# The scratch tensor u in natural order (channel, batch, time): one run of 8 KB per channel stored, each channel's rows loaded by two DMAs of 64 batches

## The reference

```
# x (64, 128, 2048); condition (64,) in 0..15; weights (16, 128, 128); length (64,)
W = weights[condition]
u = x + einsum('bct,bcd->bdt', x, W)        # a 128x128 matrix per batch mixes the channels
dt = exp(log_dt);  A = -exp(log_A_real) + 1j*A_imag;  dtA = A*dt
Ct = (C[...,0] + 1j*C[...,1]) * (exp(dtA) - 1)/A
K  = 2*real(einsum('hn,hnl->hl', Ct, exp(dtA[:,:,None]*arange(2048))))   # one long filter per channel, 64 modes
y  = causal_convolution(u, K) + u*D[:,None]  # along time, done with an FFT
out = u + y * (arange(2048) < length[:,None])[:,None,:]
```

## Time and profile before

| | us |
|---|---|
| median of three runs | 1077.04 |
| lowest and highest run | 1073.87, 1077.26 |
| span of the profiled execution | 1073.5 |
| mixing stage, DMA-paced part | 18 to about 250 |
| last batches of mixing, paced by PE | 250 to 313 |
| hand-over from mixing to the main stage | 313 to 334 |
| first slots, with the stores of kept halves | 334 to 402 |
| steady slots | 402 to 1050 |

### The profile page before, as it was taken

One profiled execution on the slowest core, in us unless ns is written; L12 is line 12 of the kernel. 1 busy time (PEld: TensorE's weight loads), 2 busy tenths in 40 slices (PEclk: granted clock), 3 DMA queues, 4 the chain that ended last, 5 costly groups with the idle time before them and its releaser, 6 DMA issues.

```text
span 1073.5 us, 30051 instructions
## 1 busy us (share of the span) xinstructions
PE 1004.2 (94%) x11612; PEld 741.1 (69%) x11612; DVE 717.1 (67%) x1647; ACT 580.4 (54%) x1230; POOL 654.8 (61%) x1377
## 2 busy tenths in 40 slices
PE   7977779778999999999999999999999999999998
PEld 4333234233347887888888888888888888888886
DVE  3988950000006877788788788778778778888875
ACT  2643444344535555566566556556655656656654
POOL 3211051201207887888888888888888888888740
PEclk9999999899999999999999999999999999999999
DMA  8999999999989999999999999999999999999994
GB/s 323 424 421 424 423 422 423 363 424 424 424 314 326 292 281 261 252 230 229 232 225 234 223 233 235 224 234 222 230 224 225 226 212 250 224 223 229 237 220 124
DMA packets 169630, 305.01 MB, mean 284 GB/s; under 512 B 78274, under 2 KB 111426, under 8 KB 161298
## 3 DMA queue, kind: packets, MB, share of 16 engines
q1 hardware_dynamic: 169170, 302.64, 98.5%
q0 software_dynamic: 160, 0.20, 0.1%
q10 hardware_dynamic: 160, 0.26, 0.1%
HBM read 152.37 MB, written 134.41 MB: 267 GB/s over the span
## 4 chain that ended last, share of the span: by engine, by line
PE 77%; DMA 17%; ACT 3%; issue 2%; DVE 0%; SPq 0%; ACTq 0%
PE bank L603 16%; DMA u_scratch<-stage 15%; PE bank L617 15%; PE bank L570 14%; PE bank L556 11%; PE bank L544 9%; PE bank L582 7%; PE bank L609 5%; ACT stage L743 2%; DMA x_f<-in_x 1%; DMA gt_sb<-g_sb 0%; ACT ring L743 0%; DMA u_row<-u_scratch 0%; DMA u_scratch<-ring 0%; DVE st_sb L1039 0%
## 5 line engine op out<-in xcount | busy, mean ns | idle before, releaser
L603 PE MATMUL bank<-toep,u_t 128*128 128x192 f16 (+1 forms) x3072 | 342.5, 220 | 0.2
L617 PE MATMUL bank<-g_sb,st_sb 128*128 128x256 f16 x1536 | 306.0, 273 | 0.8 <-issue 0.8
L544 PE MATMUL bank<-x_f,w_buf 128*128 128x512 f32 x512 | 243.0, 621 | 52.1 <-ACT stage L743 29.0
L556 PE MATMUL bank<-ident,u_row 128*128 128x128 f32 x1024 | 277.5, 275 | 4.4 <-DMA u_row<-u_scratch 1.7
L773 ACT ACTIVATE st_sb<-bank 128x128 f16<-128x128 f32 x448 | 123.8, 276 | 256.3 <-PE bank L582 194.1
L603 PEld LDWEIGHTS bank<-toep,u_t 128*128 128x128 f16 x3072 | 231.4, 99 | 13.7
L544 PEld LDWEIGHTS bank<-x_f,w_buf 128*128 128x128 f32 x512 | 95.9, 196 | 190.3 <-issue 116.7
L1057 DVE COPY_PREDICATED o_sb<-mask,u_row 128x512 f32<-128x512 uint8 x256 | 212.5, 830 | 16.6 <-issue 16.5
L1034 DVE SCALAR_TENSOR_TENSOR u_t<-bank,u_t 128x512 f16<-128x512 f32 x256 | 176.1, 688 | 56.0 <-ACT u_t L757 56.0
L1039 DVE TENSOR_TENSOR st_sb<-bank,st_sb 128x128 f16<-128x128 f32 x448 | 130.4, 291 | 88.3 <-ACT st_sb L773 83.2
L609 PE MATMUL bank<-toep,x_t 128*128 128x64 f16 x2048 | 188.2, 193 | 0.2 <-issue 0.2
(11 more groups left out here) (135 smaller groups left out, 969.5 us busy)
## 6 DMA issues: line engine op xcount, KB each, us to landing
x_f<-in_x SPq DMA_DIRECT2D x64, 1024.0 KB, 19.6
u_row<-u_scratch SPq DMA_DIRECT2D x128, 512.0 KB, 5.9
out<-o_sb SPq DMA_DIRECT2D x254, 256.0 KB, 3.8
u_scratch<-stage SPq DMA_DIRECT2D x48, 1024.0 KB, 17.7
toep<-k_scratch SPq DMA_DIRECT2D x64, 256.0 KB, 6.1
u_scratch<-ring SPq DMA_DIRECT2D x14, 512.0 KB, 14.6
u_scratch<-kept SPq DMA_DIRECT2D x12, 448.0 KB, 6.5
gt_sb<-g_sb SPq DMA_TRANSPOSE x124, 5.4
```

The lines of the kernel that those rows point to most:

```text
L544: last = pe.matmul(bank[:, 4 * (n % 2) + k, :], w_buf[n % XS][:, :], x_f[n % XS][:, k * 512:(k + 1) * 512], start=True, stop=True)
L556: last = pe.transpose(bank[:, 4 + q, g * P:(g + 1) * P], u_row[c % 4][:, h, g, tb * P:(tb + 1) * P], ident[:, :])
L603: pe.matmul(bank[:, y, col + tb * P + NM:col + Q], u[:, h, tb, a, rows_], t[:, h, b, NM:Q - tb * P], start=first, stop=False, skip_group_c ...
L617: last = pe.matmul(bank[:, y, col:col + Q], st[:, h, a, gr * ROWS:(gr + 1) * ROWS], g[:, h, b, :], start=False, stop=(m == 2), skip_group_ ...
```

## The change

The scratch tensor becomes [H, NB, T]: for each channel 64 batches of 2048 time steps. A whole batch is stored as one run of 8 KB per channel. A half is still 4 KB per channel. A head's rows, which used to be one block of 512 KB, are now loaded by two DMAs, each for 64 partitions: the first half of time of all batches, then the second, in runs of 4 KB that lie 8 KB apart. The semaphore of a head's load is raised by 32 instead of 16, and PE waits for 32 times the round.

```diff
-    u_dram = nc.dram_tensor("u_scratch", [H, ROWS, NG, Q], F32, kind="Internal")
+    u_dram = nc.dram_tensor("u_scratch", [H, NB, T], F32, kind="Internal")
             def store_u(n, s):
-                dst = bass.AP(u_dram, n * NG * Q, [[ROWS * NG * Q, H], [NB * NG * Q, JJ], [1, NG * Q]])
-                sp.dma_start(dst, stage[n % STAGES][:, :, :, :].rearrange("p j a t -> p j (a t)")).then_inc(s, 16)
+                sp.dma_start(u_dram[:, n, :], stage[n % STAGES][:, :, :, :].rearrange("p j a t -> p (j a t)")).then_inc(s, 16)
             def store_half(n, j, first, last, s):
-                dst = bass.AP(u_dram, (first * ROWS + j * NB + n) * NG * Q, [[ROWS * NG * Q, last - first], [1, NG * Q]])
-                sp.dma_start(dst, half_buffer(n, j)[first:last, :, :].rearrange("p a t -> p (a t)")).then_inc(s, 16)
+                sp.dma_start(u_dram[first:last, n, j * NG * Q:(j + 1) * NG * Q], half_buffer(n, j)[first:last, :, :].rearrange("p a t -> p (a t)")).then_inc(s, 16)
             def load_u(i, c, h):
                 wait(sp, s_ov, 4 * (UN * i + c - 4) + 2 * h + 2)
-                sp.dma_start(u_row[c % 4][:, h, :, :].rearrange("p g q -> p (g q)"),
-                             bass.AP(u_dram, (2 * (UN * i + c) + h) * (ROWS * NG * Q), [[NG * Q, ROWS], [1, NG * Q]]))\
-                    .then_inc(s_row[c % 4][h], 16)
+                for j in range(JJ):
+                    sp.dma_start(u_row[c % 4][j * NB:(j + 1) * NB, h, :, :].rearrange("p g q -> p (g q)"),
+                                 u_dram[2 * (UN * i + c) + h, :, j * NG * Q:(j + 1) * NG * Q]).then_inc(s_row[c % 4][h], 16)
                 if k % 8 == 0:
-                    pe.wait_ge(s_row[c % 4][k // 8], 16 * (i + c // 4 + 1))
+                    pe.wait_ge(s_row[c % 4][k // 8], 32 * (i + c // 4 + 1))
```

## The result

| | before | after |
|---|---|---|
| median of six runs, us | 1075.59 | 1083.99 |
| lowest to highest | 1071.38 to 1077.43 | 1080.04 to 1087.58 |
| span of the profiled execution | 1073.5 | 1077.9 |

The changed kernel is slower by 0.8%: the ratio is 1.0082, with a 95% interval of 1.0058 to 1.0106. The median of before moved from 1077.04 to 1075.59 us with three more runs. The profiled execution of after belongs to its lowest run (1080.04 us), so the two spans differ by less, 4.4 us, than the medians, 8.4 us.

The account below looks back on a forecast made before the run. Stores through the queue were taken to bound the first 250 us, PE the main stage. Stores -2.1 us and split loads +2.3 us (1.2 + 0.5 + 0 + 0.6) gave +0.2 us, forecast 1077.3 us, range 1072.5 to 1088.

Parts of the forecast that it names:

- rival B: Loads at the start: isolated half-load price everywhere, hand-over paying it; +3.5 us, 1080.5 us, 1086 at 0.8 a head; chance 0.22.
- Part 1: Mixing stage: 8 KB stores instead of twice 4 KB win 2.1 us, bounds 0.4 and 3.8.
- Part 2: Head loads by two 64-partition DMAs: 0.58 us more each in an empty queue, 0.3 in a full one.
- hand-over with slot 1: Pair 0's two heads land 1.2 us later; three further heads in a full queue cost 0.5 us.
- The second DMA's issue is within this: Hand-over: issuing each head's second DMA adds nothing beyond 0.58 us a head; two loads issue in 0.81 us.
- Slots 1 to 5: Slots up to 400 us: 11 more heads need 3.3 us of queue time, covered by 3.9 us idle; cost 0.
- the term for 400 us: After SP's wait for the kept halves: one load into an empty queue, on PE's path, 0.6 us more.
- SP has room too: Steady slots: SP stands idle 3.3 us and gets two more issues a slot, at most 0.8 us.
- Steady slots: Main loop: two heads a slot add 0.6 to 1.16 us of queue time within 1.45 us of room; cost 0.
- Rival C: Main loop: the queue becomes the bound of the steady slots; +28 us, 1105 us at 0.9 us a head; chance 0.12.
- rival A: Head loads: halves are free and part 1 stands alone; -3.8 us with its full 10 ns, 1073.2 us; chance 0.20.
- full price of 1.28 us a head: Head loads at a fully halved rate: upper bound of 1.28 us a head, in all +76 us; given little chance.

Follow-up runs that it names:

- e9: Changed kernel, but a whole batch stored by two DMAs, one per half of time, so packets are 4 KB at the new addresses; ratio 1.0148.
- e10: Changed kernel, but ACT's queue issues the second half-load of each head of pairs 0 to 7; ratio 1.0069.
- e1: Kernel before with its old scratch layout, each head loaded by two DMAs of 64 partitions in a row; ratio 1.0072, median 1088.17 us.
- b0: Kernel before run again without edit, on another chip; ratio 1.0014.
- e2: Kernel before with its old layout, each head loaded by two DMAs, even partitions then odd ones; ratio 1.0024, median 1083.38 us.
- e12: Kernel before with even and odd partition loads as in e2, but ACT's queue issues the odd ones for pairs 0 to 7; ratio 1.0028.
- e4: Kernel before, heads loaded by two DMAs of 64 partitions only from pair 9 on; ratio 0.9976 (0.9941 to 1.0011).
- e11: Kernel before plus one tiny DMA (4 bytes to each of 128 partitions) on SP behind each head's load of pairs 0 to 8; ratio 1.0024.
- e5: Kernel before, heads loaded by two DMAs of 64 partitions for pairs 0 to 8 only, single loads later; ratio 1.0121, median 1091.83 us.
- e0: Changed kernel run again without edit; ratio 1.0078.
- e3: Changed kernel with a whole batch written as two adjacent 4 KB runs in one DMA, which were joined to 8 KB packets; ratio 1.0104.
- e7: Changed kernel, but channels 0 to 15 keep the old layout, with their own store DMA and single loads for pairs 0 to 7; ratio 1.0082.

## Why the prediction was right or wrong

The forecast was 1077.3 us, within 0.3% of before; measured is 1083.99 us, in the range, but slower by 0.8%. That is the place of rival B (1080.5 to 1086 us, chance 0.22), not of the forecast's case.

**Part 1 was right in size, and in mechanism as far as the runs can tell.** Predicted were 2.1 us from 5.4 ns a packet, between bounds of 0.4 and 3.8. The store period fell from 4.944 to 4.907 us in the median (0.038 us x 44 batches = 1.7 us), with 4 KB packets at the new addresses it was 4.95 (e9), and mixing ended 2.1 us earlier on average over all profiles; e10's period of 4.963 is the exception. There is a slip in the working: with the same 9 ns for the smallest packets the second pair of equations gives 153.6 and 308.0 ns, so that two of 4 KB cost 0.8 ns less than one of 8 KB, not 1 ns more. The middle would have been 4.7 ns and 1.8 us. That the truth lies near the middle is luck: nothing in the rows had chosen it. The assumption that a store's packet of 8 KB costs what a load's does fits this size. In the first profile mixing ended 2.9 us earlier, of which about 2 can be put down to the packets and the rest to the scatter of one execution.

**Part 2: the price "0.58 us a head in an empty queue" was mis-sized, and two terms were missing.** For the hand-over with slot 1 the sum said 1.2 + 0.5 = 1.7 us; the second L570 group came 3.6 us later than before (25.8 against 22.2 us after the end of mixing). What failed is the step from 255 and 182 ns to 73 ns a packet. Both prices were read in windows in which the queue was partly empty (shares of 68.0% and 88.8%). In the full queue of the hand-over a packet took 293 ns on one side against at most 168 (e1, b0), and the second head landed 2.3 us later than before, 1.1 a head and not 0.58. Of these 2.3 us, 1.5 are the side of the partitions (10.6 in e1 against 9.1 in e2) and 0.8 the second DMA as such (9.1 against 8.3), which had no term. The other missing term is the clock: behind the longer wait came 3.4 us at 1.2 GHz, some 0.8 us at the first mark. The sentence "The second DMA's issue is within this" held, although a load of 64 partitions takes SP 0.60 us to issue: with the second issues moved to ACT (e10, e12) the heads landed no earlier.

**Slots 1 to 5 cost little, as said.** Predicted 0, measured 0.6 us between the second mark and the sixth (47.5 against 46.9 us), about the scatter.

**Slots 5 to 8: the term for 400 us was mis-sized, and the barrier was taken to stay where it was.** Predicted 0.6 us for one load in an empty queue; measured 2.8 us between the sixth and the ninth mark (39.0 against 36.2), and 4.5 against b0. Counted from the end of mixing, the 7.0 us at the ninth mark are 4.6 us by which the last kept half lands later (92.0 against 87.3), 2.0 us by which the load of pair 8 takes longer behind it (5.4 us from issue to landing against 3.4; e1 has 4.7 and e2 4.2, but e4, which loads this head whole, 4.6), and 0.4 us behind that, where the clock is down. In after the barrier moves with PE, which is 4.2 us late by the sixth mark. In e2 and e11 it does not: there PE is on time at the sixth mark (68.6, 69.0) and the last kept half still lands 4.6 and 3.2 us later than in before. So a second DMA a head delays the stores ahead of the barrier also by itself. "SP has room too" was read off a steady slot, and SP is much fuller while it issues the kept halves; but whether its time is the reason, or the extra transfers in the queue, is open, as e12 was late with an SP that had room.

**Steady slots: right.** Predicted 0, measured 0.3 us over 55 slots; e4 shows the same with its own ratio. Rival C (halves as the bound of the main loop) did not come: the share rose by 3 points, 0.35 us a slot, under the 1.45 us of room worked out from the earlier trace rows. The mean 4 KB packet from 500 to 1000 us, loads and stores together, was 225 ns in the traces of before and of after. The prediction named that as a sign of rival A; it came, and A was wrong for the start. A price read in one state of the queue did not hold in another.

**The rivals and the full price.** A (free halves) fell with e1. B is nearest in the sum, and with its 0.8 us a head also at the hand-over (3.6 us). But it put 4.9 us into the slots up to 400 us by queue time, where PE lost 0.6, and it had the barrier's delay and the clock as little as the forecast had. The Trainium skill's rule, in "SBUF — State Buffer", section on the DMA port swizzle, that 64 partitions in a row reach half the ports, agrees with e1 against e2: with both sides in each DMA a packet took 190 ns, on one side 284, and 293 in the fullest stretch. A strict halving of the rate would be 319 ns, an estimate: twice the 159.5 ns worked out from the earlier trace rows. So the full price of 1.28 us a head, which the forecast discounted, was the nearer one at the hand-over (1.0 us from the packets, 1.1 from the landings). The rule of "DMA: Bandwidth & Descriptors", rules for kernel authors, to use one transfer of 128 partitions, held as it stands: every version with halves in the first slots lost 0.7% or more.

**Open.** What delays the kept halves in e2, e11 and e12, SP's time or the additional transfers in the queue, was not separated. Why PE pauses in the steady slots without a wait that the profile shows, and most in e5, is not known. e9's ratio is not explained by its marks alone.

## What to carry to other kernels

A DMA that is split can cost in three ways: if each part takes 64 partitions in a row, its packets; the second transfer itself, even when it moves next to nothing; and, if PE waits for it, a stretch at half the clock behind the wait. Read the price of a packet where the queue is as full as it will be at the place that counts. Look at what stands ahead of a barrier: a delay of the stores there comes back whole in everything behind it. A layout that saves packets on one side is worth what a packet costs (some 5 ns for each pair of 4 KB joined here), which is little beside a dependent load that comes a microsecond later.

## What the runs showed of the hardware

- With two 4 KB packets joined to one of 8 KB a saturated batch of 2 MB took 4.907 us in the median instead of 4.944 (three profiles of four; the fourth, e10, has 4.963).
- A packet of 4 KB from 6 to 9 us after the end of mixing: 279 to 284 ns in loads of 64 partitions in a row (after, e1), 190 ns with every second partition (e2), 161 to 169 ns with all 128 (b0, before). With the queue full, 229 against 408 GB/s.
- Behind waits of PE of 2.35 us (after), 2.40 (e0) and 2.48 (e1) the granted clock was 1.2 GHz for 3.4 us; behind waits of 2.40 (e3), 2.57 (e9) and 2.63 us (e10) at the same place it stayed at 2.4 GHz.
- Issuing the second half from ACT's queue did not bring the one-sided halves to full rate: the second head landed 10.7 us after the end of mixing, against 10.6 from one queue and 9.1 with even and odd rows (e2).
- With 128 KB of each 1 MB store sent from 16 partitions by a DMA of its own, a batch took 5.12 us in the median (e7) instead of 4.91 to 4.94.
- 128 packets of 4 bytes ahead of a load delayed its landing by 1.8 us, of which 0.46 us were the later issue (e11).
- Two 4 KB runs side by side on both ends of one DMA were sent as one packet of 8 KB (e3).
